# Slot table of an expert layer: column comparisons in one VectorE operation, token numbers multiplied in by ScalarE

## The reference, cut to what matters

```
logits = flat @ router_w.T
probs = softmax(logits)
topk_probs, topk_idx = top_k(probs, 2)
topk_probs = topk_probs / (sum(topk_probs) + 1e-09)
y[n, e] = w2[e] @ (silu(w1[e] @ flat[n]) * (w3[e] @ flat[n]))
out = einsum('ne,nec->nc', gates, y)
```

## Time and profile before

| | |
|---|---|
| median of three runs | 2415.05 us (2396.78 to 2415.8) |
| profiled execution, its own time | 2420.91 us |
| its span | 2419.3 us |
| busy in the span: PE, DVE, ACT, POOL | 75%, 52%, 33%, 49% |
| mean granted clock of TensorE | 0.847 |

### The profile page before, as it was taken

One profiled execution on the slowest core, in us unless ns is written; L12 is line 12 of the kernel. 1 busy time (PEld: TensorE's weight loads), 2 busy tenths in 40 slices (PEclk: granted clock), 3 DMA queues, 4 the chain that ended last, 5 costly groups with the idle time before them and its releaser, 6 DMA issues. The chain is left out here.

```text
span 2419.3 us, 34670 instructions
## 1 busy us (share of the span) xinstructions
PE 1818.1 (75%) x10022; PEld 1444.7 (60%) x10023; DVE 1260.5 (52%) x3894; ACT 795.5 (33%) x1606; POOL 1178.5 (49%) x1121
## 2 busy tenths in 40 slices
PE   3365666656657776777677698968479999999996
PEld 3243554444544444445444487857368888888885
DVE  7454555555545545455455376655944444444442
ACT  4122222222212222222222156855034444444442
POOL 1576666776766665656666100022034444444443
PEclk8588778788778777888888799955789999999998
DMA  7555556565545555555555354646713322232222
GB/s 238 175 191 178 183 187 204 169 209 183 193 160 196 182 169 188 191 182 188 185 193 195 97 168 167 230 139 188 289 32 46 49 44 44 46 48 46 44 45 34
DMA packets 142044, 356.62 MB, mean 147 GB/s; under 512 B 33130, under 2 KB 79625, under 8 KB 127611
## 3 DMA queue, kind: packets, MB, share of 16 engines
q0 software_dynamic: 66624, 157.12, 25.0%
q1 hardware_dynamic: 69068, 198.31, 23.2%
q10 hardware_dynamic: 6255, 0.10, 0.3%
HBM read 297.49 MB, written 57.94 MB: 147 GB/s over the span
## 5 line engine op out<-in xcount | busy, mean ns | idle before, releaser
L190 POOL DMA_INDIRECT gathered<-xn_rows,src_table x832 | 843.9, 1014 | 431.9 <-issue 250.9
L795 PE MATMUL bank<-edge_attr,dst_select 128*128 128x256 f32 x1664 | 553.4, 504 | 393.5 <-ACT edge_attr L723 209.5
L795 PEld LDWEIGHTS bank<-edge_attr,dst_select 128*128 128x128 f32 x1664 | 425.8, 263 | 518.7 <-ACT edge_attr L723 230.0
L1783 PE MATMUL bank<-rowsT_parts,expert_weights 128*128 128x256 f16 x3564 | 409.3, 274 | 10.1 <-issue 6.3
L614 DVE TENSOR_SCALAR dst_select<-iota_window,dst_partition 128x128 f32<-128x128 f32 x832 | 257.0, 310 | 288.0 <-DMA gathered<-xn_rows,src_table 235.3
L1783 PEld LDWEIGHTS bank<-rowsT_parts,expert_weights 128*128 x3564 | 346.8, 98 | 59.0 <-issue 18.1
L723 ACT ACTIVATE edge_attr<-edge_attr 128x2048 f32<-128x2048 f32 x104 | 198.3, 1906 | 457.2 <-DVE edge_attr L625 312.8
L625 DVE TENSOR_TENSOR edge_attr<-gathered,edge_attr 128x256 f32<-128x256 f32 x832 | 344.1, 414 | 0.0
L1744 POOL DMA_INDIRECT out<-expert_out,output_row_of_slot x108 | 183.1, 1696 | 301.1 <-ACTq L1842 278.6
L1889 DVE SCALAR_TENSOR_TENSOR gated<-bank,silu 128x512 f32<-128x512 f32 x216 | 120.6, 558 | 184.9 <-ACT silu L1828 173.7
L635 DVE SCALAR_TENSOR_TENSOR node_sum<-bank,in_first_tile,node_sum 128x256 f32 x104 | 49.8, 479 | 308.7 <-PE bank L795 173.6
(11 more groups left out here) (273 smaller groups left out, 1978.4 us busy)
## 6 DMA issues: line engine op xcount, KB each, us to landing
edge_attr<-in_edge_attr SPq DMA_DIRECT2D x104, 1024.0 KB
raw_weights<-in_L_ffn_w SPq DMA_DIRECT2D x32, 544.0 KB, 4.6
expert_weight_parts<-weight_parts SPq DMA_DIRECT2D x32, 544.0 KB, 3.1
expert_weights<-expert_weight_parts SPq DMA_DIRECT2D x8, 2176.0 KB, 25.5
gathered<-xn_rows,src_table POOLq DMA_INDIRECT x832
rows_in<-xn_rows SPq DMA_DIRECT2D x48, 128.0 KB
rows_in<-in_x SPq DMA_DIRECT2D x48, 128.0 KB
residual_rows<-residual_tile SPq DMA_DIRECT2D x48, 128.0 KB
```

The costliest lines, as they stand in the source:

```text
L190: pool.indirect_dma_start(out=k.GA[h][:, e, :], out_offset=None, in_=k.xn_d[:, :], in_offset=bass.IndirectOffsetOnAxis(ap=k.src[:, b, e:e ...
L795: last = pe.matmul(WINP[b % 2][:, 0:C], SEL[b % 3][:, e, :], EA[b % 3][:, e, :], start=e == 0, stop=e == EK - 1)
L1783: last = pe.matmul(bank[:, jj * TT:(jj + 1) * TT], w(e, wp, at + b * step, 128), X16[h][:, xp, b, :], start=n == 0, stop=n == 3 * CB - 1)
```

## The change

One more pair of buffers, IDS, is added, of the shape of LANE. COL no longer carries the token's number but only the comparison, and all five pairs of a group are compared by one VectorE operation over 125x570 elements. ScalarE multiplies each pair's LANE tile with the token's number plus one, one activation for each pair, 125x128 elements, with the number as the scale operand of each partition. TensorE takes IDS as stationary operand and waits for ScalarE's new semaphore `ids_done` in place of `select_done`. ScalarE waits for `select_done`, and from the third group on for `select_used`, which it also finds in VectorE's wait. What VectorE waits for stays as it was, and the number of buffers is two for each tile.

```diff
     LANE = [sb(f"slot_lane_select{h}", [TR, GP, 128], F32, st) for h in two]
-    COL = [sb(f"slot_column_token{h}", [TR, GP, SLOTS], F32, st) for h in two]
+    IDS = [sb(f"slot_lane_token{h}", [TR, GP, 128], F32, st) for h in two]
+    COL = [sb(f"slot_column_select{h}", [TR, GP, SLOTS], F32, st) for h in two]
...
@@ scalar
                 act.dma_start(k.tok_d..., extra[:, :, :]).then_inc(extra_out, 16)
+            act.wait_ge(ready, 7)
+            for n in range(NG):
+                act.wait_ge(select_done, n + 1)
+                if n >= 2:
+                    act.wait_ge(select_used, n - 1)
+                for j in range(GP):
+                    c = n * GP + j
+                    last = act.activation(IDS[n % 2][:, j, :], LANE[n % 2][:, j, :], ACT.Copy, scale=idf[:, c // 2:c // 2 + 1])
+                last.then_inc(ids_done, 1)
             act.wait_ge(extra_out, 16)
@@ tensor
             for n in range(NG):
-                pe.wait_ge(select_done, n + 1)
+                pe.wait_ge(ids_done, n + 1)
                 for j in range(GP):
-                    last = pe.matmul(INV, LANE[n % 2][:, j, :], COL[n % 2][:, j, :], ...)
+                    last = pe.matmul(INV, IDS[n % 2][:, j, :], COL[n % 2][:, j, :], ...)
                 last.then_inc(select_used, 1)
@@ vector
             for n in range(NG):
                 if n >= 2:
                     dve.wait_ge(select_used, n - 1)
-                for j in range(GP):
-                    c = n * GP + j
-                    ts(COL[n % 2][:, j, :], iol[0:TR, 0:SLOTS], column[:, c:c + 1], idf[:, c // 2:c // 2 + 1], ALU.is_equal, ALU.mult)
+                tt(COL[n % 2][:, :, :], iol[0:TR, 0:SLOTS].unsqueeze(1).to_broadcast([TR, GP, SLOTS]),
+                   column[:, n * GP:(n + 1) * GP].unsqueeze(2).to_broadcast([TR, GP, SLOTS]), ALU.is_equal)
                 tt(LANE[n % 2][:, :, :], iol[0:TR, :].unsqueeze(1).to_broadcast([TR, GP, 128]),
                    lane[:, n * GP:(n + 1) * GP].unsqueeze(2).to_broadcast([TR, GP, 128]), ALU.is_equal).then_inc(select_done, 1)
```

More of the change, by code:

```diff
@@ L1486, in dispatch_stage @@
         "route_consts", "logits_shifted", "exp_done", "ranks_full", "extras_done", "extras_out"))
-    select_done, select_used = sem("slot_select_done"), sem("slot_select_used")
+    select_done, ids_done, select_used = sem("slot_select_done"), sem("slot_ids_done"), sem("slot_select_used")
     INV = k.psum[0][:, 0:SLOTS]
@@ L1529, in _ @@
             for n in range(NG):
-                pe.wait_ge(select_done, n + 1)
+                pe.wait_ge(ids_done, n + 1)
                 for j in range(GP):
-                    last = pe.matmul(INV, LANE[n % 2][:, j, :], COL[n % 2][:, j, :], start=n == 0 and j == 0, stop=n == NG - 1 and j == GP - 1)
+                    last = pe.matmul(INV, IDS[n % 2][:, j, :], COL[n % 2][:, j, :], start=n == 0 and j == 0, stop=n == NG - 1 and j == GP - 1)
                 last.then_inc(select_used, 1)
```

## The result

The changed kernel took 2421.77 us (median of 19 runs, 2395.5 to 2434.03), the kernel before 2404.8 us in its 19 runs (2396.12 to 2419.22). The ratio is 1.0047, 95% interval [1.0024, 1.007]: slower by 0.47%, 11 us, with 6 to 17 us inside the interval. A ratio in this document compares the means of the executions at the usual speed (here 16 of the changed kernel's 19, mean 2417.5 us, with all 19 of the kernel before, mean 2406.3 us; the three left out took 2432.8 to 2434.0 us), so it is not the quotient of the two medians, 1.0071. The two kernels' spreads overlap widely, so single runs say nothing. Everything the change touches lies in one loop, which every trace shows to 0.01 us.

A forecast was written before the change was run, and what follows sets the result against it. VectorE bounds the dispatch loop before; afterwards two buffers make each round the sum of VectorE, ScalarE, TensorE and hand-overs, 4.545 us. The table is read 7.2 us later: 2415.05 + 7.2 = 2422 us, range 2400 to 2436 us.

The forecast's parts named there:

- The bound of the kernel before: Dispatch-stage loop: VectorE sets the pace without gaps, 1.982 us a group, with one wait of 0.60 us.
- VectorE's saving: Dispatch loop: one 570-element comparison replaces five operations; VectorE's group takes 1.405 us in place of 1.982.
- ScalarE's cost: Dispatch loop: 100 added activations of 388 ns each, starting 293 ns apart; five last 1.56 us.
- The ring: Dispatch loop: two buffers keep two groups in flight, so a round sums three engines' legs: 4.545 us, 2.27 a group.
- The clock: TensorE's leg in the dispatch loop: 2.48 us at half clock first, 1.37 at full clock after one halfway round of 5.10.
- The first rival: Dispatch loop: two groups in flight, TensorE stays at half clock, rounds 5.655 us; +16.6 us, 2431.7 us; chance 0.15.
- The rise at the head: Start of the dispatch loop: TensorE's first two groups, 4.4 us at a stretch, raise its clock as before.
- The rival without a ring: Dispatch loop: buffers do not bind, ScalarE sets the pace at 1.47 us a group; 9.8 us earlier, 2405 us; chance 0.10.
- The total: Whole kernel: +7.2 us from the dispatch loop, 2422 us; within 1% given 0.90.

The follow-up runs named there:

- the spare product: Changed kernel with one more TensorE product of two constant 128x128 tiles into an unused bank behind each group; loop 49.26 us, ratio to the kernel before 1.0006.

## Why the prediction was right, and where its size was off

- **The bound of the kernel before** was VectorE: right. A third buffer moved that loop by 0.7 us.
- **VectorE's saving** was priced right: 754 ns for 570 elements where 737 was forecast, and 1.41 us a group. The saving shows only once there are more buffers.
- **ScalarE's cost** was right: 386 ns for one, 1.57 us for five, where 388 ns and 1.56 us were forecast. By the Trainium skill (ScalarE: Activation LUTs, What ACT_TABLE_LOAD costs) the estimate was 386 ns, which is what the trace has. The same page of the Trainium skill (Rules for kernel authors) says to use VectorE for a multiplication, with its speed in bf16 as the reason; the tiles here are fp32. Following that rule keeps the loop as it was (42.16 us): with two buffers that was the better choice (55.82 us), with three the move pays (35.18 us).
- **The ring** was right: 5.66 us a round at half clock (5.655 forecast), 4.55 at full clock (4.545), shown by the spare product. With a third buffer it still binds, with three groups in a round of 4.55 us in place of two.
- **The clock** was the mis-sized term. The sum took TensorE's leg at 2.48 us for the first round and from then on, after one round in between, at 1.37 us. In three executions of the changed kernel the clock was at half for most of the loop, TensorE's leg there was 2.5 us, and most rounds lasted 5.66 us (about half of them in the execution of 54.84 us). The first rival (ring with a low clock, priced at +16.6 us, given 0.15) was what mostly happened: +13.7, +12.7 and +16.3 us over 42.16. The spare product shows that this term was the clock's alone: with it gone, 49.26 us stand beside the 49.3 us forecast.
- **The rise at the head.** It was argued that the first two groups would bring the clock up as before. In the trace above two groups back to back (4.62 us) did not, and the first rise, later, was lost again behind the next stretch. In the execution of 58.50 us they did, and it was lost just as soon, so the step that failed is that a risen clock would stay. The first rival's picture of the low clock was off too: it had TensorE pause 1.3 us in each round of 5.7, and the trace has 0.55 us in 5.66. At full clock the ring leaves TensorE busy 2 x 1.37 of 4.55 us; the argument leaned on the row with 2.19 of 3.41 us, which is a busier stretch than that.
- **The rival without a ring** (2405 us) was refuted by the 17 waits of VectorE for TensorE. Three buffers brought 1.52 us a group, near the ScalarE pace that it described (1.47), by a longer ring and not by its absence.
- **The total.** The ratio's interval, 0.24% to 0.70%, holds both the 7.2 us forecast (0.30%) and the 13.7 us seen in the trace (0.57%). Within 1% was right. The time itself landed closer than the reasoning deserves, as said above.

## What to carry to other kernels

When a step is handed to another engine, count the engines between the first write of a buffer and its release, and add up the legs: with b buffers a group costs at least that sum divided by b, however idle each engine is. With three buffers that rule gave 4.55 / 3 = 1.52 us, as measured. A stage more in the chain wants a buffer more; here the third one turned 0.47% slower into about 0.4% faster. Then ask what the new pauses do to TensorE's clock, since its leg at half clock is part of the same sum and can keep itself there.

## What the runs showed of the hardware that was not expected

A TensorE clock that had risen did not last in a ring which the higher clock itself made emptier. In the changed kernel the granted clock went up for 3.41 us, TensorE was busy 1.72 us of it, and the clock went back to 0.50; behind a later rise it stayed up over a stretch with 1.80 us busy in 3.41, but in the three executions no rise inside the loop lasted longer than 6.8 us. With the order of VectorE's operations changed, rounds of 3.95 us with 1.34 us of products a group ran at full clock to the end. With the spare product, 1.37 + 0.40 us of products in half a round of 4.55 us did too. Adding work to TensorE made the loop 6.6 us shorter.
